# Chunks of 128 queries instead of 256 in a fused attention and FP4 feed-forward kernel, with a reordered head

## The chip, the cores and the metric

The kernel runs on one core of one Trainium2 chip. The metric is the device time of the whole program in microseconds. Engines: TensorE (PE, with its weight loads as PEld), VectorE (DVE), ScalarE (ACT), GpSimd (POOL), and SyncE (SP), which only issues transfers.

## The reference, cut to what matters

Sequence 2048, width 128, 16 heads of 8 features; all in float32.

```
x_proj = silu(x @ W1 + b1);  u, v, q, k = split(x_proj, 4)
attn   = silu(q k^T per head) / S            # no softmax, no mask
av     = attn v
y      = layernorm(av * u, gamma, beta) @ W2 + b2
x      = layernorm(x + y)
gate   = fp4(x) @ fp4(w_gate).T;  up = fp4(x) @ fp4(w_up).T      # 352 columns
h      = silu(gate) * up
out    = layernorm(x + fp4(h) @ fp4(w_down).T)
```

`fp4` quantises blocks of 16 numbers to a grid of eight magnitudes, scaled by the largest of the block.

## The kernel before, in words

**The attention.** The queries are cut into chunks (`WIDTHS`, eight of 256), and each chunk into steps (`STEPS`, 256 in all). A step has one tile of 128 keys and four head groups' worth of work, 512 columns in each of four PSUM banks: with 256 queries a step covers two of the four values of m and a chunk has 32 steps; with 128 queries it would cover all four and a chunk would have 16. Either way there are 256 steps with two ACTIVATEs (silu) of 128x1024 each.

In each step TensorE does, in this order: `scores(at)`, which is a half a=0 and a half a=1, each with bf16 matmuls of 64 rows in pairs on the two halves of the array (eight of 256 columns in a step); `times_v(at - 2)`, fp32 matmuls with 32 output columns in four column groups (sixteen records of 256 columns in a step); and then the job that `JOB_AT` has for that step, if any. A half of scores waits until ScalarE has emptied the bank pair that was used three halves ago (`SB = 3`). `times_v` waits for the ACTIVATEs of its own step.

**Jobs.** `PREP_AT` places the remaining projections (k, v, u, q), the folding of gamma and beta into W2, and the transposes of the quantised weights in steps 0 to 33. `PAIR_JOBS` places, behind the attention of the next chunk, the rest of the network for the two tiles of a finished chunk: "y" (step base + 0), "xqT" (+5), "gate" for each tile (+6, +7), "up" (+8, +9), "hqT" (+14, +15), "down" for both (+16). `PAIR_BASE` = 45, 68, 100, ... 228. A job waits until the job before it has been taken from PSUM: by ScalarE (the silu of k, q, v, u and of each "gate") or by VectorE (all others). ScalarE does its part of job(at) between its two ACTIVATEs of step at + 1. VectorE does layer norms (with a reciprocal root from GpSimd), quantisation and copies, two tiles interleaved.

**Head.** `HEAD` lists what TensorE does before step 0: transposes of x into xT and the first projections, in an order written out by hand. Biases of q and k are loaded one number to a partition by ScalarE's queue (`load_bias`), before and after the half of W1 that q and k need. VectorE permutes the columns of that half (L828). Features are split into three bf16 parts (`split`), and transfers by SyncE and GpSimd (`stack`, L231) put these into `k_stack` and `q_stack`, whose unused rows are zeroed by large transfers (`zero_rows`, L222). Step 0 waits for all of xT and for the stacks of k 0 and q 0; steps 2, 6, 10 and 14 wait for the stack of a further unit of k.

**Tail.** After the last step the last two tiles go through the whole remaining network with nothing beside them; matmuls on zeros (`KEEP_WARM`) fill TensorE's waits.

## Time and profile before

| | |
|---|---|
| median of 3 runs | 555.74 us (555.68 to 562.42) |
| the profiled execution: its own time | 553.78 us |
| its span, first to last instruction | 551.9 us |
| granted TensorE clock, mean over the span | 1.00 (2.4 GHz) |
| first attention ACTIVATE starts | 22.04 us |
| last attention ACTIVATE ends | 524.90 us |
| steps | 256, with 512 attention ACTIVATEs |

The span has three parts: a head of 22 us until the first ACTIVATE of the attention, 503 us of steps, and a tail of 27 us. Starts in the timeline are microseconds from the span's start. ACTIVATEs that follow each other overlap in the record, so their rate is read from the ends of blocks of them. Matmul records overlap too, so TensorE's steps are read from the starts of successive blocks.

### The profile page before, as it was taken

The numbers are of one execution on the slowest core, as the hardware profiler recorded it, in microseconds if no ns is written. First come the engines' busy times: TensorE is split into PE (matmuls) and PEld (weight loads), VectorE is DVE, ScalarE is ACT, GpSimd is POOL, SyncE is SP. The second block draws the span as 40 slices with busy tenths as digits, with TensorE's granted clock in tenths as the row PEclk, the third lists the DMA queues.
The fourth block names the chain that finished last, engine by engine and source line by source line (L and its number), as shares of the span: only waits on it lengthen the run. The fifth ranks groups of instructions, "written<-read, shape, count | busy, mean of one in ns | idle before, by whom it ended". The sixth has DMA issues, their size and how long they took to land.

```text
span 551.9 us, 15085 instructions
## 1 busy us (share of the span) xinstructions
PE 514.1 (93%) x6586; PEld 227.7 (41%) x6586; DVE 180.2 (33%) x610; ACT 494.3 (90%) x559; POOL 60.6 (11%) x151
## 2 busy tenths in 40 slices
PE   4699999999999999999999999999999999999996
PEld 2344444344443433434343433444343443444343
DVE  3652742043322510452023510452023510442046
ACT  2699999999999999999999999999999999999910
POOL 5840000020120010201020010201010010201021
PEclk9999999999999999999999999999999999999999
DMA  8780240000000000000000000000000000000000
GB/s 171 199 162 17 72 106 11 2 2 1 11 2 2 1 11 2 1 3 11 1 3 1 2 11 1 3 2 12 1 2 1 1 12 1 2 2 11 3 0 11
DMA packets 13993, 12.08 MB, mean 22 GB/s; under 512 B 2019, under 2 KB 13286, under 8 KB 13926
## 3 DMA queue, kind: packets, MB, share of 16 engines
q1 hardware_dynamic: 12790, 9.05, 6.8%
q0 software_dynamic: 704, 1.92, 1.5%
q8 instruction: 52, 0.85, 0.6%
q10 hardware_dynamic: 432, 0.13, 0.2%
q14 instruction: 15, 0.12, 0.1%
HBM read 1.92 MB, written 1.05 MB: 5 GB/s over the span
## 4 chain that ended last, share of the span: by engine, by line
ACT 43%; PE 30%; issue 11%; DVE 8%; POOL 4%; DMA 2%; ACTq 1%; DVEq 0%; POOLq 0%
ACT attn L573 41%; PE ps L363 28%; POOL rstd_a L357 2%; DMA b_col<-in_L_attn_b 2%; POOL rstd_b L357 2%; PE ps L507 1%; POOL ve_a L356 1%; DVE mv_a L745 1%; DVE x_b L748 1%; DVE stats_a L743 1%; DVE amax_a L712 1%; POOL ve_b L356 0%; PE ps L502 0%; ACT feat L573 0%; ACT gate_b L573 0%
## 5 line engine op out<-in xcount | busy, mean ns | idle before, releaser
L573 ACT ACTIVATE attn<-ps 128x1024 f32<-128x1024 f32 x512 | 478.2, 1146 | 18.1 <-PE ps L363 17.9
L363 PE MATMUL ps<-attn,v_pad 128*32 128x256 f32 x4096 | 273.9, 385 | 0.8 <-ACT attn L573 0.5
L363 PE MATMUL ps<-q_stack,k_stack 64*128 64x256 bf16 x2048 | 178.2, 274 | 14.7 <-ACT attn L573 0.9
L363 PEld LDWEIGHTS ps<-attn,v_pad 128*32 128x32 f32 x4096 | 107.1, 109 | 98.9 <-issue 53.4
L363 PEld LDWEIGHTS ps<-q_stack,k_stack 64*128 64x128 bf16 x2048 | 67.4, 94 | 154.0 <-ACT attn L573 115.9
L356 POOL TENSOR_TENSOR ve_a<-mv_a,eps_col 128x1 f32<-128x1 f32 x24 | 4.5, 189 | 466.3 <-DVE mv_a L745 466.3
L739 DVE SCALAR_TENSOR_TENSOR zu<-ps,uT 128x256 f32<-128x256 f32 x8 | 3.4, 423 | 121.5 <-PE ps L363 121.5
L743 DVE BATCH_NORM_STATS2 stats_a<-ps 128x6 f32<-128x128 f32 x8 | 2.4, 300 | 57.6 <-PE ps L363 57.6
L795 DVE TENSOR_TENSOR gate_a<-gate_a,ps 128x352 f32<-128x352 f32 x7 | 3.7, 522 | 50.6 <-PE ps L363 50.6
L363 PE MATMUL ps<-zeros 128*128 128x512 bf16 x75 | 18.3, 396 | 1.2 <-DVE zeros L818 1.2
L363 PE MATMUL ps<-xT,w_qk 128*128 128x512 f32 (+1 forms) x20 | 10.2, 606 | 7.9 <-DVE w_qk L828 5.5
L363 PE MATMUL ps<-wup_t,xqT 128*128 128x352 f32 x32 | 13.4, 505 | 1.8 <-ACT gate_b L573 1.8
L363 PE MATMUL ps<-wgate_t,xqT 128*128 128x352 f32 x32 | 13.4, 505 | 1.8 <-ACT gate_a L573 1.8
L680 DVE CAST parts<-feat 128x512 bf16<-128x512 f32 (+1 forms) x10 | 4.8, 476 | 30.7 <-ACT feat L573 30.7
L573 ACT ACTIVATE feat<-ps,b_col 128x512 f32<-128x512 f32 (+1 forms) x10 | 7.0, 697 | 7.5 <-PE ps L363 5.6
L357 POOL TENSOR_TENSOR rstd_b<-ve_b,minus_half 128x1 f32<-128x1 f32 x24 | 13.2, 551 | 1.9
L357 POOL TENSOR_TENSOR rstd_a<-ve_a,minus_half 128x1 f32<-128x1 f32 x24 | 13.2, 549 | 1.9
L363 PEld LDWEIGHTS ps<-zeros 128*128 128x128 bf16 x75 | 7.4, 101 | 9.8 <-issue 1.4
L641 ACT ACTIVATE xqT<-ps 128x128 f32<-128x128 f32 x2 | 0.5, 277 | 10.6 <-PE ps L554 10.6
L722 DVE TENSOR_TENSOR xn_a<-xn_a,magic_a 128x352 f32<-128x352 f32 (+3 forms) x21 | 8.5, 403 | 0.2
L721 DVE TENSOR_TENSOR xn_a<-xn_a,magic_a 128x352 f32<-128x352 f32 (+3 forms) x21 | 8.4, 401 | 0.2
L363 PEld LDWEIGHTS ps<-wup_t,xqT 128*128 128x128 f32 x32 | 4.9, 188 | 8.5 <-ACT gate_b L573 5.2
(152 smaller groups left out, 326.0 us busy)
## 6 DMA issues: line engine op xcount, KB each, us to landing
k_stack<-parts SPq DMA_DIRECT2D x18, 128.0 KB, 3.3
q_stack<-parts SPq DMA_DIRECT2D x18, 128.0 KB, 2.4
k_stack<-uT POOLq DMA_DIRECT2D x2, 448.0 KB, 7.8
q_stack<-uT SPq DMA_DIRECT2D x2, 448.0 KB, 8.2
x_sb<-in_L_attn_x SPq DMA_DIRECT2D x3, 256.0 KB, 6.9
k_stack<-parts SPq DMA_DIRECT2D x10, 64.0 KB, 3.1
q_stack<-parts SPq DMA_DIRECT2D x8, 64.0 KB, 2.0
out<-x_a SPq DMA_DIRECT2D x8, 64.0 KB, 1.5
```

What stands on the lines that cost most here:

```text
L356: link(pool.tensor_tensor(r.ve[:, :], r.mv[:, which, 1:2], eps_col[:, :], ALU.add))
L357: pool.tensor_tensor(r.rstd[:, which:which + 1], r.ve[:, :], minus_half[:, :], ALU.pow).then_inc(rstd_ready, 1)
L363: return pe.matmul(to, lhsT, rhs, start=start, stop=stop, skip_group_check=True)
L507: last = pe.transpose(ps[0:fn, bank, t * P:(t + 1) * P], r.xn[:, f0:f0 + fn], ident[:, :])
L573: return act.activation(to, frm, ACT.Silu, **kw)
L680: dve.tensor_copy(p[:, 0, :], f).then_inc(split_done, 1)
L712: each(lambda t: dve.tensor_reduce(t.amax, t.src, AX_X, ALU.max, apply_absolute_value=True))
L721: each(lambda t: dve.tensor_tensor(t.xn, t.xn, t.magic, ALU.add))
L722: each(lambda t: dve.tensor_tensor(t.xn, t.xn, t.magic, ALU.subtract))
L743: dve.bn_stats(r.stats[:, :], src)
L745: dve.bn_aggr(r.mv[:, which, :], r.stats[:, :]).then_inc(var_ready, 1)
L748: return dve.tensor_scalar(to, src, r.mv[:, which, 0:1], r.rstd[:, which:which + 1], ALU.subtract, ALU.mult)
```

## The change

- Sixteen chunks of 128 queries, sixteen steps each. A step has sixteen score matmuls of 128 columns and thirty-two records of `times_v` with 128 columns.
- One tile of 128 rows passes behind the attention beside each chunk from the second on: fifteen tiles, "y", "xqT", "gate", "up", "hqT", "down" at steps 3, 7, 9, 11, 15 and 17 from the chunk's first (the fifteenth tile: 2, 6, 8, 10, 14, 15). VectorE works on one tile at a time. The last tile alone makes the tail, with 27 and 22 zero matmuls in place of 33 and 28.
- The weights' transposes move to steps 14 to 21; the projections of q 512, 1024, 1536 and of u 1, 2, 3 move to steps 29 to 69, one for each half chunk. VectorE's program for the first chunk is laid out by steps (`QUANTISE_AFTER`).
- The head: b1 is loaded as rows on one partition, permuted by VectorE and turned into columns by three matmuls against a one; ScalarE permutes W1 in place of VectorE, and its queue issues only the load of W1's half; the columns 256 to 767 of `k_stack` are zeroed by a GpSimd memset, the rest by transfers that GpSimd issues only after its shares of the first two stacks; the order of `HEAD` has all transposes of x before v 0 and k 768.
- SyncE stacks q 512 and later units between the writes of the output.

```diff
-WIDTHS = (256,) * 8
+WIDTHS = (128,) * 16
-    KEEP_WARM = {"y": 5, "xqT": 33, "gate": 2, "hqT": 28, "down": 2}
+    KEEP_WARM = {"y": 5, "xqT": 27, "gate": 2, "hqT": 22, "down": 2}
-    PREP_AT = {0: ("k", 1280), 1: ("v", 1), 3: ("k", 1792), 5: ("v", 2), 8: ("v", 3), 10: ("u", 0),
-               12: ("q", 256), 14: ("u", 1), 16: ("q", 512), 18: ("u", 2), 20: ("u", 3), 22: ("q", 1024),
-               24: ("q", 1536), 27: ("w2", 0), 29: ("gate", 0), 31: ("up", 0), 33: ("down", 0)}
-    PAIR_BASE = [45, 68, 100, 132, 164, 196, 228]
-    PAIR_JOBS = {0: ("y", 0), 5: ("xqT", 0), 6: ("gate", 0), 7: ("gate", 1), 8: ("up", 0), 9: ("up", 1),
-                 14: ("hqT", 0), 15: ("hqT", 1), 16: ("down", 0)}
+    PREP_AT = {0: ("k", 1280), 1: ("v", 1), 3: ("k", 1792), 5: ("v", 2), 7: ("v", 3), 9: ("u", 0), 11: ("q", 256),
+               14: ("w2", 0), 16: ("gate", 0), 18: ("up", 0), 21: ("down", 0), 29: ("q", 512), 37: ("u", 1),
+               45: ("q", 1024), 53: ("u", 2), 61: ("q", 1536), 69: ("u", 3)}
+    QUANTISE_AFTER = {3: "gate", 7: "up", 11: "down"}
+    TAIL = KT - 1
+    TILE_AT = {t: (BEGIN[t + 1], {"y": 3, "xqT": 7, "gate": 9, "up": 11, "hqT": 15, "down": 17}) for t in range(TAIL - 1)}
+    TILE_AT[TAIL - 1] = (BEGIN[TAIL], {"y": 2, "xqT": 6, "gate": 8, "up": 10, "hqT": 14, "down": 15})
-        HEAD = [("xT", 0, 256, 0), ("k", 0, 256, 1), ("q", 0, 256, 2), ("xT", 256, 512, 3), ("k", 256, 512, 4),
-                ("v", 0, 512, 6), ("xT", 768, 512, 5), ("k", 768, 512, 7), ("xT", 1280, 512, 7),
-                ("xT", 1792, 256, 7)]
+        HEAD = [("xT", 0, 256, 0), ("k", 0, 256, 1), ("q", 0, 256, 2), ("xT", 256, 512, 3), ("xT", 768, 512, 4),
+                ("k", 256, 512, 5), ("xT", 1280, 512, 7), ("xT", 1792, 256, 0), ("v", 0, 512, 6),
+                ("k", 768, 512, 7)]
...
+            sp.dma_start(b1_natural[0:1, 0:2 * D], b1[2 * D:4 * D].rearrange("(a n) -> a n", a=1)).then_inc(b1_rows_loaded, 16)
+            sp.dma_start(b1u_row[0:1, 0:D], b1[0:D].rearrange("(a n) -> a n", a=1)).then_inc(b1_rows_loaded, 16)
...
+            pool.memset(k_stack[:, :, :].bitcast(F32)[:, :, 128:384], 0.0).then_inc(k_early_zeroed, 1)
...
+            pool.wait_ge(zero_row_ready, 1)
+            zero_rows(pool, k_stack, 768, k_rest_zeroed)
+            pool.wait_ge(b1v_ready, 1)
+            zero_v(0)
...
+            pe.wait_ge(b1_permuted, 1)
+            for i, row in enumerate((b1u_row[0:1, 0:D], b1_permuted_row[0:1, 0:D], b1_permuted_row[0:1, D:2 * D])):
+                last = mm(ps[:, 6, i:i + 1], row, ones_row[0:1, 0:1])
+            last.then_inc(b1_made, 1)
...
-                load_bias(2, b1k_loaded)
-                act.dma_start(w1_sb[:, 2 * D:4 * D], W1[:, 2 * D:4 * D]).then_inc(w1_kq_loaded, 16)
-                load_bias(1, b1_loaded)
+            act.dma_start(w1_sb[:, 2 * D:4 * D], W1[:, 2 * D:4 * D]).then_inc(w1_kq_loaded, 16)
...
+            def permute_w1(i):
+                src = w1_sb[:, (2 + i) * D:(3 + i) * D].rearrange("k (h s d) -> k h d s", h=2, d=HD)
+                to = w1_qk[:, i, :].rearrange("k (h d s) -> k h d s", h=2, d=HD)
+                act.activation(to, src, ACT.Copy).then_inc(w1_qk_ready, 1)
...
+            def to_quantised_x(tile):
+                r = ROWS[tile % 2]
+                bank = wait_made("y", 0, tile)
+                statistics(ps[:, bank, 0:P], 0, r)
+                y_plus_x(r, ps[:, bank, P:2 * P], tile).then_inc(job_by_vec, 1)
+                wait_taken("y", 0, tile)
+                statistics(r.x1p[:, :], 1, r)
+                quantised_x([r])
...
+            def to_out(tile):
+                r = ROWS[tile % 2]
+                bank = wait_made("down", 0, tile)
+                dve.tensor_tensor(r.x1p[:, :], ps[:, bank, 0:D], r.x1[:, :], ALU.add).then_inc(job_by_vec, 1)
+                wait_taken("down", 0, tile)
+                statistics(r.x1p[:, :], 2, r)
+                finish(tile)
```

## Rows read from the trace of the kernel before

**Rows 1.** The page: busy time of each engine; engines of the chain that ended last.

```profile
PE 514.1 (93%) x6586; PEld 227.7 (41%) x6586; DVE 180.2 (33%) x610; ACT 494.3 (90%) x559; POOL 60.6 (11%) x151
...
ACT 43%; PE 30%; issue 11%; DVE 8%; POOL 4%; DMA 2%; ACTq 1%; DVEq 0%; POOLq 0%
```

**Rows 2.** Timeline of ACT, one pair: start us, us, what, count [idle before].

```profile
234.22 1.02 ACT L573 ACTIVATE attn<-ps 128x1024 f32<-128x1024 f32 x1 [0.21 <-PE ps L363]
...
235.48 1.03 ACT L573 ACTIVATE attn<-ps 128x1024 f32<-128x1024 f32 x1
236.88 1.02 ACT L573 ACTIVATE attn<-ps 128x1024 f32<-128x1024 f32 x1 [0.36 <-PE ps L363]
...
241.87 12.94 ACT L573 ACTIVATE attn<-ps 128x1024 f32<-128x1024 f32 x14 [0.39 <-PE ps L363]
255.78 6.52 ACT L573 ACTIVATE attn<-ps 128x1024 f32<-128x1024 f32 x7 [0.98 <-PE ps L363]
```

**Rows 3.** Timeline of PE over the same pair: steps, and three jobs.

```profile
221.63 0.33 PE L502 MATMUL ps<-ident,zu 128*128 128x128 f32 x1
...
222.45 0.61 PE L363 MATMUL ps<-q_stack,k_stack 64*128 64x256 bf16 x8
...
224.00 0.61 PE L363 MATMUL ps<-q_stack,k_stack 64*128 64x256 bf16 x8
...
232.99 0.86 PE L363 MATMUL ps<-wgate_t,xqT 128*128 128x352 f32 x2
233.78 0.61 PE L363 MATMUL ps<-q_stack,k_stack 64*128 64x256 bf16 x8
...
253.81 0.94 PE L363 MATMUL ps<-wdown_t,hqT_a 128*128 128x128 f32 x6
...
255.35 0.61 PE L363 MATMUL ps<-q_stack,k_stack 64*128 64x256 bf16 x8
```

**Rows 4.** Timeline of PE in the head: a projection, then 128-column matmuls.

```profile
14.04 1.13 PE L363 MATMUL ps<-xT,w_qk 128*128 128x512 f32 x2 [1.72 <-ACT xT L604]
15.00 1.05 PE L363 MATMUL ps<-w_sb,xT 128*128 128x128 f32 x8
```

**Rows 5.** By tile, 100 to 500 us: min/median/max ns of the attention's matmuls (two answers).

```profile
L363 PE MATMUL ps<-q_stack,k_stack x1640: 268/270/282, 100.8 to 499.4; 64*128 64x256 bf16 x183
...
L363 PE MATMUL ps<-attn,v_pad x3288: 378/379/404, 99.8 to 499.9; 128*32 128x256 f32 x194
```

**Rows 6.** Timeline of PEld: the eight weight loads of one step's scores.

```profile
301.31 0.33 PEld L363 LDWEIGHTS ps<-q_stack,k_stack 64*128 64x128 bf16 x8 [0.49 <-issue]
```

**Rows 7.** Timeline of DVE: first and last instruction from "y" to quantised x.

```profile
222.56 0.30 DVE L743 BATCH_NORM_STATS2 stats_a<-ps 128x6 f32<-128x128 f32 x1 [5.86 <-PE ps L363]
...
230.67 0.29 DVE L725 TENSOR_TENSOR xn_b<-xn_b,scale_b 128x128 f32<-128x128 f32 x1
```

**Rows 8.** Timeline of the head, all engines.

```profile
0.74 1.90 ACTq L578 DMA_DIRECT2D b_col<-in_L_attn_b  x2
...
2.68 0.46 ACTq L582 DMA_DIRECT2D w_sb<-in_L_attn_W  x1
...
8.93 0.59 DVE L828 COPY w_qk<-w_sb 128x64 f32<-128x64 f32 x4 [5.37 <-DMA w_sb<-in_L_attn_W]
...
13.02 0.47 ACT L573 ACTIVATE feat<-ps,b_col 128x256 f32<-128x256 f32 x1 [1.90 <-DMA b_col<-in_L_attn_b]
...
14.12 2.35 POOL L231 DMA_DIRECT2D q_stack<-parts  x4 [0.17 <-issue]
...
22.04 2.85 ACT L573 ACTIVATE attn<-ps 128x1024 f32<-128x1024 f32 x3 [0.49 <-PE ps L363]
```

**Rows 9.** Timeline of the last steps and the tail.

```profile
515.49 9.41 ACT L573 ACTIVATE attn<-ps 128x1024 f32<-128x1024 f32 x10
...
539.17 0.52 DVE L712 TENSOR_REDUCE amax_a<-gate_a 128x22 f32<-128x352 f32 x1
...
544.62 0.53 DVE L725 TENSOR_TENSOR xn_b<-xn_b,scale_b 128x352 f32<-128x352 f32 x1
```

More of the change, by code:

```diff
@@ L96, in build, with chunk_of @@
     job_no = {job: k for k, job in enumerate(JOBS)}
[L97 to L98 removed]
+    ACT_JOBS = [k for k, (kind, i, tile) in enumerate(JOBS)
+                if kind in ("k", "q", "v", "u") or (kind == "gate" and tile is not None)]
     VEC_JOBS = [k for k in range(len(JOBS)) if k not in ACT_JOBS]
[L100 to L104 removed]
+    def chunk_of(tile):
+        return max(c for c in range(len(WIDTHS)) if Q0[c] <= tile * P)
     UNITS = [("k", 0, 256), ("q", 0, 256), ("k", 256, 512), ("k", 768, 512), ("k", 1280, 512), ("k", 1792, 256),
@@ L175, in build @@
         ROWS = [Rows([sb(f"{name}_{k}", shape) for name, shape in shapes.items()]) for k in "ab"]
+        TAIL_ROWS = [ROWS[tile % 2] for tile in range(TAIL, KT)]
         xqT = sb("xqT", [D, 2, P])
@@ L269, in _, with write_out @@
             sp.wait_ge(q_rest_zeroed, 32)
-            for n in range(unit_no[("q", 256)], len(UNITS)):
-                stack(sp, n)
-            for n in range(KT):
-                sp.wait_ge(x2_ready, n + 1)
-                sp.dma_start(out_v[:, n, :], ROWS[n % 2].x2[:, :]).then_inc(out_written[n % 2], 16)
+            stack(sp, unit_no[("q", 256)])
+            def write_out(tile):
+                sp.wait_ge(x2_ready, tile + 1)
+                sp.dma_start(out_v[:, tile, :], ROWS[tile % 2].x2[:, :]).then_inc(out_written[tile % 2], 16)
+            for at in sorted(JOB_AT):
+                kind, start, tile = JOB_AT[at]
+                if kind == "q" and start > 256:
+                    stack(sp, unit_no[("q", start)])
+                elif kind == "down" and tile is not None:
+                    write_out(tile)
+            write_out(TAIL)
             for k in range(2):
@@ L472, in job @@
                     pe.wait_ge(av_taken, STEPS[at - LAG][0])
-                if p is not None:
-                    last = behind(kind, i, p, bank)
+                if tile is not None:
+                    last = behind(kind, tile, bank)
                 elif kind == "u":
@@ new lines, in finish @@
+            def finish(tile):
+                r = ROWS[tile % 2]
+                dve.wait_ge(rstd_ready, rstd_no.next())
+                if tile >= 2:
+                    dve.wait_ge(out_written[tile % 2], 16 * (tile // 2))
+                normalise(r.x1p[:, :], r.x2[:, :], 2, r).then_inc(x2_ready, 1)
+            def to_quantised_x(tile):
+                r = ROWS[tile % 2]
+                bank = wait_made("y", 0, tile)
[4 more added lines that the diff above has]
+                quantised_x([r])
@@ new lines, in _ @@
+            for at in range(len(STEPS)):
+                if at - LAG in BEGIN[1:]:
+                    take_av(BEGIN.index(at - LAG) - 1)
+                kind, start, tile = JOB_AT.get(at, (None, None, None))
+                if tile is None:
+                    if kind in ("k", "q"):
+                        split(kind, start)
+                    elif kind == "w2":
+                        take_w2()
+                    elif kind in ("gate", "up", "down"):
+                        take_weights(kind)
+                elif kind == "y":
+                    to_quantised_x(tile)
+                elif kind == "xqT":
+                    copy_xqT(tile)
+                elif kind == "up":
+                    to_quantised_h(tile)
+                elif kind == "hqT":
+                    copy_hqT(tile)
+                elif kind == "down":
+                    to_out(tile)
+                if at in QUANTISE_AFTER:
+                    quantise_weights(QUANTISE_AFTER[at])
@@ L908, in _ @@
                 statistics(r.x1p[:, :], 2, r)
-            finish(LAST)
+            for i in range(KT - TAIL):
+                finish(TAIL + i)
 _INS = ["L0_attn_x", "L0_attn_W1", "L0_attn_b1", "L0_attn_W2", "L0_attn_b2", "L0_attn_gamma", "L0_attn_beta",
```

317 lines of the change are left out of this document (138 added, 179 removed).

## The prediction

> **What bounds the kernel now.** I read the page first: PE is busy for 93% of the span and ACT for 90%, and the chain that ended last alternates between them [rows 1]. That average does not say which waits for which, so the timeline of ACT comes next, over one pair of tiles (they repeat seven times). In an unbroken block, fourteen ACTIVATEs take 12.94 us, the first of them 1.02: (12.94 - 1.02) / 13 = 0.917 us each [rows 2]. 512 at that pace are 469 us, and nothing in the change touches it. What can be won lies outside: the head of 22.04 us until the first ACTIVATE [rows 8], the tail from 524.90 (515.49 + 9.41) to 551.9 [rows 9], and what interrupts ACT between. The first ACTIVATE ends about 1.02 after its start, at 23.06, so from there to 524.90 are 501.8 us; 511 x 0.917 = 468.3, which leaves 33.5 us of interruptions.
>
> Their kinds are seen in the same block of rows, by ends. 235.24 to 236.51 is 1.27 us, 0.35 more than the pace: the silu of "gate" that lies between, ACT's own work. 236.51 to 237.90 is 1.39, 0.47 more: a wait for PE. Six ACTIVATEs end between 235.24 and 242.89, 7.65 us, which is 2.15 over the pace: two silus (0.70) and three waits of 0.47 to 0.50 (1.45). One wait of about 0.3 stands ahead of them, and at "down" the end moves from 254.81 to 256.80, a wait of 1.07 [rows 2]. A pair thus costs 2.8 us of waits and 0.7 of silus, seven pairs 24.5. The other 9.0 lie in the first 40 steps, mostly ACT's own part of the projections.
>
> Why ACT waits is in PE's timeline. A step in which PE waits for nothing lasts 222.45 to 224.00, 1.55 us (1.544 over several), while ACT needs 2 x 0.917 = 1.833 [rows 2, 3]. PE gains 0.29 per step and loses the length of a job where one stands: "y" for two tiles 0.82, "gate" 0.79, "down" for two tiles 1.54 (253.81 to 255.35) [rows 3]. Call what PE is behind its best place the backlog. "y" with 0.82 stops ACT not at all; before "down" two "hqT" of 0.48 stand, so the backlog reaches 0.48 - 0.29 + 0.48 - 0.29 + 1.54 = 1.92, and ACT waits 1.07. So the three score buffers forgive about 0.83, and the wait is what exceeds that. Two "gate" and two "up" in four successive steps exceed it each time. Over all 256 steps this rule gives about 35 us of interruptions where the trace has 33.5, close enough to use.
>
> **The change, part by part.** *Width.* The columns streamed per step stay the same, so a gain is excluded; the number of matmuls and loads doubles. No row shows a bf16 matmul of 128 columns. Near to it are the fp32 records of 128 columns, each with a load of 128 columns of its own: eight in 1.05 us, the last 0.28, so (1.05 - 0.28) / 7 = 0.11 us each [rows 4], which is 128 columns passed twice at 2.4 GHz (0.107) and 3 ns; the load is hidden entirely. What a load costs when nothing hides it can be read from the longest matmul against the median: 12 ns for scores, 25 for times_v [rows 5], little against 56 and 110 ns of streaming. I take 3 ns per additional matmul: scores go from 4 x 0.110 to 8 x 0.056, times_v from 4 x 0.216 to 8 x 0.110, together 0.02 to 0.03, and a free step is 1.57. The lower end is 1.55. For the upper end I take the loads as they appear in a full step: eight in 0.33 us, 0.041 each [rows 6]. If the two of a pair had to run one after the other with no overlap of the matmul, a pair would last 0.083, eight 0.66, and the step 1.77.
>
> The Trainium skill ("TensorE: Matmul & The Clock Gate", section on the back-to-back issue gap) speaks against the change: it gives about 81 ns for each matmul of 128 columns in a sustained stream of loads and matmuls, against 56 for one without a load. The fp32 row above has no such addition, but its matmul is twice as long; by the page the scores would cost 8 x 0.025 = 0.2 us more and the step would be about 1.77, an estimate.
>
> *Jobs of one tile.* By records of 0.11 and 0.15 for the change of layout: "y" 0.82 - 0.33 = 0.49, "xqT" 0.26, "gate" and "up" 0.79 each as before, "hqT" 3 x 0.11 + 0.15 = 0.48, "down" 1.54 - 0.66 = 0.88; together 3.7. A chunk then asks 16 x 1.57 + 3.7 = 28.8 us of PE and 32 x 0.917 + 0.35 = 29.7 of ACT: ACT still sets the pace. With two steps between "gate" and "up" and four or more elsewhere, every job starts with little or no backlog; 0.88 after "hqT" exceeds the cushion (0.82 now) by 0.07, everything else by nothing. Fifteen tiles cost 15 x 0.07 = 1 us of waits and 15 x 0.35 = 5.3 of silus.
>
> *The last tile behind the attention* has "y" one step earlier, only one after the preceding tile's "down", and VectorE must first finish that tile (add, statistics, root, normalise) and take the chunk: about 2.6 us, against 1.57. PE waits about 1.1 us in its queue, with the scores of the next step behind it; backlog 0.6 + 1.1 + 0.49, minus 0.82, is a wait of 1.3. Its adjacent "hqT" and "down" add 0.3.
>
> *The moved projections.* One lasts 15.00 - 14.04 = 0.96 and 0.10 for layout, 1.06 [rows 4]. In the first chunks before, they stood every second step, each hidden by ACT's own work for the one before. Alone, half a chunk apart, each meets a backlog of 0.25 from the tile's job ahead: 1.31 - 0.82 = 0.5, six times 3.0. The v and k jobs of steps 0 to 9 stay about as they were, 2.0. ACT's own share of all projections is unchanged, 6.8.
>
> *Sum of interruptions:* waits 1.0 + 1.6 + 3.0 + 2.0 = 7.6, ACT's own 6.8 + 5.3 = 12.1; 19.7 against 33.5, a gain of 13.8.
>
> *Head.* W1's half for q and k is issued at 2.68 and VectorE gets it at 8.93 [rows 8], 6.2 us later. With the bias loads gone it is issued in place of the first of them, at 0.74, 1.9 earlier, and the 1.90 that ACT waited for the bias of q at 13.02 is gone too. The features of q then end near 10.3 in place of 13.5, and SyncE's and GpSimd's stacks (2.35 us of issue for GpSimd's share) with them. ScalarE pays for it with two permutations of some 0.35 us, ahead of xT. Next late is PE: all transposes, k 256, v 0 and k 768 add to 5.9 us after q, with handovers 6.5, which gives scores near 16.2 and the first ACTIVATE at 16.6 in place of 22.04: a gain of 5.4. Ends: 2 (loads land no earlier) and 7. On the other side, k_stack's rows from 768 are zeroed only after GpSimd's stacks, and SyncE's queue holds the stack of k 768 and all behind it until then; the W loads and v are late against earlier steps. I put 1 us on that, with ends 0 and 5.
>
> *Tail.* One tile in place of two. From the last ACTIVATE to the end are 27.0 us. The quantisation of h for two lasts 539.17 to 545.15, 5.98 [rows 9]; for one, the same nine durations with 0.03 between are 3.95: 2.0 gained. The same way the quantisation of x gains 0.6, the interleaved statistics 0.9, one multiplication 0.6, the second "gate" ahead of the first "up" 0.7, and the second tile's last normalisation, later than the first's, 0.8; minus overlaps and 0.5 that "down" may hold VectorE before the last take, 4.9. Ends 3.5 and 5.5.
>
> *Total:* 551.9 - 13.8 - 5.4 + 1 - 4.9 = 528.8 of span. The profiled execution took 553.78, 1.9 above its span, which gives 530.7; the median lay 2 us above the profiled execution, and I take 531.5 for the new median.
>
> **The rivals.**
>
> *Narrow loads are not hidden.* With a step of 1.77, PE asks 16 x 1.77 + 3.7 = 32.0 per chunk, 2.3 more than ACT, and PE is the bound: about 35 us over the forecast in fifteen chunks, 566. The price begins at a step of 1.63 (where 16 steps and 3.7 make 29.7), and at about 1.72 all gains are spent. For it: rows 6 as read above, and PE's small reserve. Against it: the 12 and 25 ns [rows 5] and the fp32 records [rows 4].
>
> The rule of the Trainium skill cited above (81 ns) leads to the same 1.77 and 566, an estimate.
>
> *The single tile's chain is too long.* From "y" to quantised x two tiles take 222.56 to 230.96, 8.4 us [rows 7]. For one I count 6.3, as the second tile's operations fall out between the first's; the step of "xqT" comes 6.5 after "y" (four steps less the backlog). If the chain stayed at 8.4, PE would stand 2.0 us at each "xqT" with scores behind it: 2.0 + 0.26 - 0.82 = 1.4, fifteen times 21, so 552, no difference. What speaks for it is that each VectorE operation waits for the one before and nothing fills the gaps; against it, the root's round trip and the gaps are counted.
>
> *The head gives its gain back*: ACT starts at 16.6 but waits in steps 2 to 18 for stacks, v or quantised weights as long as it started early. 531.5 + 5.4, up to 540.
>
> **Chances.** Forecast (525 to 536) 0.55; the head's gain lost or half of some other term (536 to 544) 0.20; the chain, or PE a little over its reserve (544 to 556) 0.09; narrow loads (over 556) 0.12; better than 525 0.04. For 8 in 10 the range needs the first two and most of the third: 525 to 552. A measurement of this kernel tells 2% from no change, 544.6 below and 566.9 above; faster 0.79, within 0.13 (the third case and a third of the fourth), slower 0.08.
>
> **What would show it.** Right: free steps near 1.57 in PE's timeline; ACT in unbroken blocks of nearly a chunk, broken by the silu alone; waits of 0.5 at six projections; one wait over 1 us at step 242; the first ACTIVATE before 18 us; a tail of 22 us. Wrong: blocks of scores that last over 0.7 us where nothing holds them; PE idle before "xqT" until VectorE's last operation in every chunk; waits for transfers in the first chunk.

## The result, and the profile after

The changed kernel takes 535.57 us (median of four runs, 532.63 to 536.49), the kernel before 557.41 beside it (555.68 to 562.42): a ratio of 0.959, 95% interval 0.952 to 0.966, 22 us less. Its profiled execution took 532.63 us with a span of 530.5; 551.9 stood before. The forecast was 528.8 for the span, 531.5 for the median.

The page of the changed kernel, the rows that answer to [rows 1], and the queue that fetches instructions:

```profile
PE 511.4 (96%) x12724; PEld 378.3 (71%) x12724; DVE 210.8 (40%) x627; ACT 492.5 (93%) x558; POOL 63.3 (12%) x152
...
q8 instruction: 100, 1.64, 1.3%
...
ACT 43%; PE 42%; issue 10%; DVE 3%; POOL 1%; DMA 1%; POOLq 0%; DVEq 0%; ACTq 0%
```

TensorE has twice the instructions and 3 us less of busy time; VectorE, GpSimd and the DMAs have 5% of the chain together, where they had 14%.

Where the 21.4 us of span came from, by the three stretches of the prediction. The pace of 0.917 us per ACTIVATE is the same in both; an interruption is what the ends of successive ACTIVATEs lie apart beyond it. The prediction took 468.3 for 511 paces, and 511 x 0.917 is 468.6; to stay comparable the table and all sums of interruptions below keep its figure, so that each is 0.3 too high and the differences are not touched:

| stretch | before | after | change | forecast |
|---|---|---|---|---|
| start of the first ACTIVATE | 22.04 | 16.74 | -5.3 | -5.4 |
| interruptions of ACT | 33.5 | 21.7 | -11.8 | -13.8, and +1 given back |
| end of the last ACTIVATE to the end | 27.0 | 22.8 | -4.2 | -4.9 |

*One chunk.* Timeline of PE in the changed kernel, parts of steps 67 to 79 (start us, us, engine, line, what, count):

```profile
123.11 0.33 PE L530 MATMUL ps<-ident,zu 128*128 128x128 f32 x1
...
123.59 0.62 PE L385 MATMUL ps<-q_stack,k_stack 64*128 64x128 bf16 x16
...
125.15 0.62 PE L385 MATMUL ps<-q_stack,k_stack 64*128 64x128 bf16 x16
125.70 1.08 PE L385 MATMUL ps<-attn,v_pad 128*32 128x128 f32 x32
126.71 1.12 PE L385 MATMUL ps<-xT,w_sb 128*128 128x512 f32 x2
127.77 0.62 PE L385 MATMUL ps<-q_stack,k_stack 64*128 64x128 bf16 x16
...
134.86 0.86 PE L385 MATMUL ps<-wgate_t,xqT 128*128 128x352 f32 x2
135.66 0.62 PE L385 MATMUL ps<-q_stack,k_stack 64*128 64x128 bf16 x16
...
146.88 0.55 PE L535 MATMUL ps<-ident,xn_a 128*128 128x128 f32 x3
147.36 0.72 PE L385 MATMUL ps<-q_stack,k_stack 64*128 64x128 bf16 x16
```

The free step is 125.15 - 123.59 = 1.56 us, against 1.55 with columns twice as wide [rows 3]: twice as many loads and matmuls cost 0.01. The jobs are the distances to the scores behind them: "y" 0.48, a projection 1.06, "gate" 0.80, "hqT" 0.48.

Timeline of ACT in the changed kernel, two places in the middle, then the last two chunks and a half:

```profile
117.56 10.30 ACT L599 ACTIVATE attn<-ps 128x1024 f32<-128x1024 f32 x11
128.21 1.02 ACT L599 ACTIVATE attn<-ps 128x1024 f32<-128x1024 f32 x1 [0.35 <-PE ps L385]
...
144.19 1.02 ACT L599 ACTIVATE attn<-ps 128x1024 f32<-128x1024 f32 x1 [0.28 <-PE ps L385]
...
439.52 26.82 ACT L599 ACTIVATE attn<-ps 128x1024 f32<-128x1024 f32 x29
466.22 0.48 ACT L599 ACTIVATE gate_b<-ps 128x352 f32<-128x352 f32 x1
466.56 15.78 ACT L599 ACTIVATE attn<-ps 128x1024 f32<-128x1024 f32 x17
483.46 12.02 ACT L599 ACTIVATE attn<-ps 128x1024 f32<-128x1024 f32 x13 [1.12 <-PE ps L385]
495.36 0.48 ACT L599 ACTIVATE gate_a<-ps 128x352 f32<-128x352 f32 x1
495.70 12.05 ACT L599 ACTIVATE attn<-ps 128x1024 f32<-128x1024 f32 x13
```

Blocks of 29 where there were blocks of seven and fourteen [rows 2]. The rows at 128.21 and 144.19 are the waits at projections, 0.46 and 0.39 by the ends. The row with 1.12 idle is the last tile's "y" at step 242; by the ends, as the prediction counts, it is (483.46 + 1.02) - (466.56 + 15.78) - 0.917 = 1.22, against 1.3. Timeline of PE at that place:

```profile
482.56 0.30 PE L530 MATMUL ps<-ident,zu 128*128 128x128 f32 x1 [0.97 <-DVE zu L764]
```

TensorE stands 0.97 us in its queue for VectorE, where the prediction had 1.1.

*The head.* Rows of several engines of the changed kernel, against [rows 8]:

```profile
0.74 0.42 ACTq L601 DMA_DIRECT2D w_sb<-in_L_attn_W  x1
...
3.37 0.43 ACT L623 ACTIVATE w_qk<-w_sb 128x128 f32<-128x128 f32 x1 [0.68 <-DMA w_sb<-in_L_attn_W]
...
16.74 2.86 ACT L599 ACTIVATE attn<-ps 128x1024 f32<-128x1024 f32 x3 [0.55 <-PE ps L385]
...
22.61 1.02 ACT L599 ACTIVATE attn<-ps 128x1024 f32<-128x1024 f32 x1 [1.53 <-PE ps L385]
...
34.83 1.94 ACT L599 ACTIVATE attn<-ps 128x1024 f32<-128x1024 f32 x2 [1.48 <-PE ps L385]
```

W1's half, issued at 0.74, is usable at 3.37. Of the wait of 1.53, 0.6 is for a stack of k, which the prediction had on its list (TensorE stands 0.58 for it); kernels below that wait for no stack there still show 0.89. The 1.48 was on no list. Timeline of PE at that place:

```profile
31.04 1.08 PE L385 MATMUL ps<-attn,v_pad 128*32 128x128 f32 x32
32.05 0.34 PE L385 MATMUL ps<-q_stack,k_stack 64*128 64x128 bf16 x6
34.56 0.45 PE L385 MATMUL ps<-q_stack,k_stack 64*128 64x128 bf16 x10 [2.17 <-issue]
```

TensorE stops for 2.17 us after the sixth of sixteen score matmuls. The program has a wait before the first and the ninth, none before the seventh. ACT loses 1.58 there by the ends and 0.76 more at the next step (1.04, where four kernels without such a stop at that place have 0.28), 2.3 in all.

*The tail.* Timeline of DVE in the changed kernel: from "y" to quantised x, and the quantisation of h:

```profile
510.98 0.30 DVE L768 BATCH_NORM_STATS2 stats_b<-ps 128x6 f32<-128x128 f32 x1 [1.05 <-PE ps L385]
...
516.97 0.29 DVE L750 TENSOR_TENSOR xn_b<-xn_b,scale_b 128x128 f32<-128x128 f32 x1
...
520.12 0.52 DVE L737 TENSOR_REDUCE amax_b<-gate_b 128x22 f32<-128x352 f32 x1
...
523.65 0.53 DVE L750 TENSOR_TENSOR xn_b<-xn_b,scale_b 128x352 f32<-128x352 f32 x1
```

The chain of one tile lasts 517.26 - 510.98 = 6.28 us (forecast 6.3; two tiles took 8.4 [rows 7]), the quantisation 4.06 (forecast 3.95).

### The profile page after: what moved, and what is told of

It is laid out like the page before. It is cut to its first block, busy times and chain, and to the rows that moved or that the text cites. A ratio compares the mean times of both kernels' runs of the same rounds, so it can differ in the third digit from the quotient of the medians.

```text
span 530.5 us, 27409 instructions
## 1 busy us (share of the span) xinstructions
PE 511.4 (96%) x12724; PEld 378.3 (71%) x12724; DVE 210.8 (40%) x627; ACT 492.5 (93%) x558; POOL 63.3 (12%) x152
## 3 DMA queue, kind: packets, MB, share of 16 engines
q8 instruction: 100, 1.64, 1.3%
HBM read 1.92 MB, written 1.05 MB: 6 GB/s over the span
## 4 chain that ended last, share of the span: by engine, by line
ACT 43%; PE 42%; issue 10%; DVE 3%; POOL 1%; DMA 1%; POOLq 0%; DVEq 0%; ACTq 0%
ACT attn L599 41%; PE ps L385 39%; PE ps L535 1%; PE ps L530 1%; DMA k_stack<-parts 1%; PE ps L417 1%; ACT feat L599 0%; POOL rstd_b L373 0%; ACT gate_a L599 0%; ACT gate_b L599 0%; DVE parts L705 0%; DVE magic_b L848 0%; DVE stats_b L768 0%; POOL rstd_a L373 0%; ACT uT L599 0%
## 5 line engine op out<-in xcount | busy, mean ns | idle before, releaser
L385 PE MATMUL ps<-attn,v_pad 128*32 128x128 f32 x8192 | 276.5, 276 | 0.0
L385 PEld LDWEIGHTS ps<-attn,v_pad 128*32 128x32 f32 x8192 | 208.1, 109 | 26.6
L385 PE MATMUL ps<-q_stack,k_stack 64*128 64x128 bf16 x4096 | 170.2, 218 | 8.3 <-issue 2.2
L385 PEld LDWEIGHTS ps<-q_stack,k_stack 64*128 64x128 bf16 x4096 | 115.0, 94 | 80.9 <-ACT attn L599 42.7
L372 POOL TENSOR_TENSOR ve_b<-mv_b,eps_col 128x1 f32<-128x1 f32 x24 | 4.6, 190 | 210.5 <-DVE mv_b L770 210.5
L818 DVE TENSOR_TENSOR gate_b<-gate_b,ps 128x352 f32<-128x352 f32 x7 | 3.6, 521 | 55.3 <-PE ps L385 55.3
L385 PE MATMUL ps<-zeros 128*128 128x512 bf16 x63 | 15.7, 399 | 1.2 <-DVE zeros L839 1.2
L385 PE MATMUL ps<-wgate_t,xqT 128*128 128x352 f32 x32 | 13.7, 511 | 0.0
L705 DVE CAST parts<-feat 128x512 bf16<-128x512 f32 (+1 forms) x10 | 6.3, 632 | 14.5 <-ACT feat L599 14.5
L773 DVE TENSOR_SCALAR x_b<-x1p_b,mv_b,rstd_b 128x128 f32<-128x128 f32 x16 | 5.5, 346 | 14.9 <-POOL rstd_b L373 14.9
L773 DVE TENSOR_SCALAR x_a<-x1p_a,mv_a,rstd_a 128x128 f32<-128x128 f32 x16 | 5.5, 346 | 14.9 <-POOL rstd_a L373 14.9
```

The costliest lines, as they stand in the source:

```text
L372: link(pool.tensor_tensor(r.ve[:, :], r.mv[:, which, 1:2], eps_col[:, :], ALU.add))
L385: return pe.matmul(to, lhsT, rhs, start=start, stop=stop, skip_group_check=True)
L705: dve.tensor_copy(p[:, 0, :], f).then_inc(split_done, 1)
L773: return dve.tensor_scalar(to, src, r.mv[:, which, 0:1], r.rstd[:, which:which + 1], ALU.subtract, ALU.mult)
L818: dve.tensor_tensor(r.gate[:, :], r.gate[:, :], ps[:, bank, 0:FF], ALU.mult).then_inc(job_by_vec, 1)
```

## The experiments

My theory was that of the prediction: TensorE's backlog with a cushion of about 0.8 us decides what a job costs, narrow loads are free, the new head brings 4.4 us net. Medians of the changed kernel itself differ by 2 us from one set to the other (535.57 and 533.37), so effects of 1 or 2 us are read from the timelines. The rivals were narrow loads that cost, a chain that is too long, and a head that gives its gain back. The kernel before ran beside each set: 556.37 us beside the first four kernels, 556.14 beside the next four, 557.02 and 556.16 beside the last. Ratios are to it, with 95% intervals.

**The width alone undone.** Chunks of 256 again, one tile per sixteen steps, the new head; the tail has two tiles and its longer runs of zero matmuls.

```
-WIDTHS = (128,) * 16
+WIDTHS = (256,) * 8
-    TAIL = KT - 1
+    TAIL = KT - 2
-    TILE_AT = {t: (BEGIN[t + 1], {"y": 3, "xqT": 7, "gate": 9, "up": 11, "hqT": 15, "down": 17}) for t in range(TAIL - 1)}
+    TILE_AT = {t: (BEGIN[t // 2 + 1] + 16 * (t % 2), {"y": 3, "xqT": 7, "gate": 9, "up": 11, "hqT": 15, "down": 17})
+               for t in range(TAIL - 1)}
```

> Chunks of 256 queries as before, but everything else as after the change: one tile at a time behind the attention, a job at most every second step, the new head. As a chunk of 256 ends two tiles at once, fourteen tiles pass behind the attention and two make the tail. Theory (the gain between head and tail comes from the spacing of the jobs, and the width itself gives nothing): free steps of 1.54 us, interruptions of ACT about 20 us as after the change (21.7), the tail back at 27, so a span near 534.5 where the changed kernel's is 530.5. Rival (the narrower chunk gives the gain between): interruptions near 33 us as before and a span near 546. Second rival (narrow matmuls cost something hidden in the sum): interruptions under 16 us, a span near or under 530.

532.88 us, 0.957 (0.954 to 0.960). The span is 532.1, 2.4 less than expected: first ACTIVATE 17.34, interruptions 17.9 (between the theory's 20 and the 16 of the second rival), tail 27.5. The narrow chunks themselves thus bring the tail (4.7 us) and cost about as much in interruptions (21.7 against 17.9): a wash. The 3.8 can be found in the timelines of ACT: steps 7 and 8, with the stop of 2.17 us that only the changed kernel has, 2.4; the wait at the last "y", 1.23 against 0.20; the six projections 0.8, since they wait 0.23 to 0.38 here and 0.39 to 0.46 there; one tile fewer behind the attention, with its silu and smaller waits at "down", 0.7. Against these, steps 1 and 2 lose 1.05 more here, with TensorE at half clock from 18.1 to 24.9 us. What this experiment shares with the change, single tiles spread over sixteen steps and the head, is where nearly all of the gain lies.

**The new head alone** (all that the change does ahead of the steps), with the width, the pairs of tiles and the positions of all jobs as before; against the changed kernel:

```
-WIDTHS = (128,) * 16
+WIDTHS = (256,) * 8
...
+    PAIR_BASE = [45, 68, 100, 132, 164, 196, 228]
+    PAIR_JOBS = {0: ("y", 0), 5: ("xqT", 0), 6: ("gate", 0), 7: ("gate", 1), 8: ("up", 0), 9: ("up", 1),
+                 14: ("hqT", 0), 15: ("hqT", 1), 16: ("down", 0)}
```

> The kernel before with the new head alone. Theory: the first ACTIVATE of the attention at 16.7 in place of 22.0 us, 1 to 3 us of it given back in the first ten steps to late stacks, all later steps as before: 2.5 to 4.5 us less than before. Rival (the transfers of the first 38 us are what bounds the start, so the gain is given back): less than 1 us. Other rival (nothing is given back): 5.3 us.

549.95 us, 0.988 (0.985 to 0.991), 6.4 us less; the span 547.4 is 4.5 less. The first ACTIVATE starts at 16.59 (5.45 earlier), the interruptions are 34.5 (1.0 more, nearly all at step 2), the tail the same 26.96. So the head gives back 1.0, the figure that the prediction took. From this kernel to the one with the width undone, 549.95 to 532.88 us, the interruptions fall from 34.5 to 17.9 at the same width: that is the spacing of the jobs, with the projections moved.

**"up" right behind "gate"**, a step of distance less:

```
-    TILE_AT = {t: (BEGIN[t + 1], {"y": 3, "xqT": 7, "gate": 9, "up": 11, "hqT": 15, "down": 17}) for t in range(TAIL - 1)}
+    TILE_AT = {t: (BEGIN[t + 1], {"y": 3, "xqT": 7, "gate": 9, "up": 10, "hqT": 15, "down": 17}) for t in range(TAIL - 1)}
```

> The changed kernel with "up" one step after "gate" in place of two, for fourteen tiles. Theory (waits come from backlog beyond the score buffers' cushion of 0.82 us, and an adjacent job also waits for ACT's silu): a wait of 0.4 to 0.5 us at each, 14 x 0.47 = 6.6 us slower than the changed kernel. Rival (only the sum of PE's work per chunk counts, 28.8 us against 29.7 for ACT): no difference.

540.66 us, 0.973 (0.968 to 0.977). ACT waits 0.47 more at each of the fourteen tiles, 6.6 in all; a shorter pause at 37 us takes 1 of it back, and the span is 535.7, 5.2 more. By the rule, backlog after two jobs of 0.79 is 0.79 - 0.29 + 0.79 = 1.29, which exceeds the cushion of 0.83 by 0.46. One step of distance is worth 5 us, and the rival that only the sum of the work counts is out. The agreement to 0.01 is partly luck. Timeline of PE of this kernel:

```profile
197.58 0.62 PE L385 MATMUL ps<-q_stack,k_stack 64*128 64x128 bf16 x16
199.47 0.86 PE L385 MATMUL ps<-wup_t,xqT 128*128 128x352 f32 x2 [0.26 <-ACT gate_a L599]
```

TensorE also stands 0.26 us before each "up" until ACT has done the silu of "gate", which the rule leaves out. It leaves out the silu's 0.35 us of ACT in the same step too, which gives TensorE time, and the two nearly cancel.

**Scores cut into 64 columns**, 32 matmuls and 32 loads per step in place of 16:

```
-                            last = mm(ps[:, bank + half, k * w:(k + 1) * w],
-                                      k_stack[rows, M * a + m, i * P:(i + 1) * P],
-                                      q_stack[rows, M * a + m, Q0[c]:Q0[c] + w])
+                                lo, hi = part * (w // 2), (part + 1) * (w // 2)
+                                last = mm(ps[:, bank + half, k * w + lo:k * w + hi],
+                                          k_stack[rows, M * a + m, i * P:(i + 1) * P],
+                                          q_stack[rows, M * a + m, Q0[c] + lo:Q0[c] + hi])
```

> The changed kernel with each score matmul of 128 columns cut in two of 64, each with its own weight load (32 in a step). Theory A (a pair costs its columns and 3 ns, loads hidden): a free step of 1.60, under 3 us slower. Theory B (loads of a pair overlap each other but take 0.041 us each pair at least): scores 16 x 0.041 = 0.66, a free step of 1.77 and 30 us slower. Theory C (0.041 for each load, one after another): scores 1.3 us, a free step of 2.4 and some 200 us slower.

542.75 us, 0.975 (0.971 to 0.979). Timeline of PE of this kernel, a free step:

```profile
203.65 0.64 PE L385 MATMUL ps<-q_stack,k_stack 64*128 64x64 bf16 x32
204.22 1.08 PE L385 MATMUL ps<-attn,v_pad 128*32 128x128 f32 x32
205.24 0.64 PE L385 MATMUL ps<-q_stack,k_stack 64*128 64x64 bf16 x32
```

1.59 us: even loads followed by only 64 columns are hidden but for 0.03 per step, as theory A had it. Its "under 3 us slower" was wrong: the median is 7 us above the changed kernel's, the span 10.9. That is no regular cost. The first ACTIVATE is 1.05 later, and the interruptions are 31.4, 9.7 more. Seventeen times TensorE stops inside a block where the program has no wait, like the stop of 2.17 us above: 0.23 to 2.63 us from the start of one matmul to the next, 9.1 together. Two stretches of 3.4 us at half clock come on top, one behind the first scores and one behind the stop of 2.63.

**"xqT" a step earlier**, so that VectorE's chain is late:

```
-    TILE_AT = {t: (BEGIN[t + 1], {"y": 3, "xqT": 7, "gate": 9, "up": 11, "hqT": 15, "down": 17}) for t in range(TAIL - 1)}
+    TILE_AT = {t: (BEGIN[t + 1], {"y": 3, "xqT": 6, "gate": 9, "up": 11, "hqT": 15, "down": 17}) for t in range(TAIL - 1)}
```

> The changed kernel with "xqT" three steps after "y" in place of four, for fourteen tiles. Theory (a single tile's chain from "y" to quantised x takes 6.3 us, and the step comes about 4.8 us after "y"): PE stands 1.6 us at each "xqT", and ACT waits 1.6 + 0.26 - 0.82 = 1.0 to 1.1 us, 14 to 16 us slower than the changed kernel. Rival (the chain of one tile takes as long as that of two, 8.4, and was hidden only just): 3 us each, over 40 us slower. Rival (the score buffers cover it): no difference.

550.73 us, 0.989 (0.981 to 0.996). Timeline of PE of this kernel:

```profile
194.19 1.08 PE L385 MATMUL ps<-attn,v_pad 128*32 128x128 f32 x32
197.00 0.30 PE L550 MATMUL ps<-ident,xn_a 128*128 128x128 f32 x1 [1.73 <-DVE xn_a L750]
197.23 0.62 PE L385 MATMUL ps<-q_stack,k_stack 64*128 64x128 bf16 x16
197.78 1.40 PE L385 MATMUL ps<-attn,v_pad 128*32 128x128 f32 x32
```

TensorE stands 1.73 us in its queue with the scores behind it, and ACT loses 1.22 in each chunk that has no projection: 1.73 + 0.26 - 0.82 = 1.17 by the rule. Where a projection stands between "y" and "xqT", as in steps 55 and 71, the loss is 0.18. This is the rival of the long chain, made real: the margin in the changed kernel is less than one step. The fourth row of the fence, 1.40 for what elsewhere takes 1.08, shows more: TensorE goes to half clock behind the pause, from 198.4 to 201.8 us (mean granted clock 0.93 from 188 to 200 us), and ACT loses another 1.5 us here, and as much again near step 200, behind the same pause. Behind the eight other pauses of this length the clock stays up.

**Tile 13 a step earlier at its end**, so that the last tile's "y" finds VectorE free:

```
+    TILE_AT[TAIL - 2] = (BEGIN[TAIL - 1], {"y": 3, "xqT": 7, "gate": 9, "up": 11, "hqT": 14, "down": 16})
```

> The changed kernel with "hqT" and "down" of the fourteenth tile one step earlier (14 and 16), so that VectorE has two steps between that "down" and the "y" of the fifteenth tile. Theory: the one wait of 1.2 us at step 242 goes, 1.2 us faster. Rival (the wait is for the attention's own product, not for VectorE's queue): no difference.

531.54 us, 0.955 (0.949 to 0.961). The wait at step 242 is gone. Timeline of ACT of this kernel, one block over both chunks where the changed kernel had 1.12 idle:

```profile
466.83 27.69 ACT L600 ACTIVATE attn<-ps 128x1024 f32<-128x1024 f32 x30
```

So its cause was VectorE, still on the tile before, as TensorE's row at 482.56 has it. The edit is worth 1.2 us; the medians differ by more (4.0 and 1.8 from those of the changed kernel), and nothing shows the rest to be its doing.

**All zeroing by memset** instead of transfers of a zero row:

```
-            zero_rows(sp, q_stack, 256, q_rest_zeroed)
...
-            pool.memset(k_stack[:, :, :].bitcast(F32)[:, :, 128:384], 0.0).then_inc(k_early_zeroed, 1)
+            pool.memset(k_stack[:, :, :].bitcast(F32)[:, :, 128:512], 0.0).then_inc(k_early_zeroed, 1)
...
-            zero_rows(pool, k_stack, 768, k_rest_zeroed)
...
+            dve.memset(k_stack[:, :, 1024:1536], 0.0)
...
+            dve.memset(k_stack[:, :, 1536:2048], 0.0).then_inc(k_rest_zeroed, 1)
...
+                    for n in range(7):
+                        last = dve.memset(q_stack[:, :, 256 * (n + 1):256 * (n + 2)], 0.0)
```

> The changed kernel with all zeroing by memset (GpSimd and VectorE, in stretches where they idle) in place of transfers, 1.5 MB of the about 5.5 MB that move in the first 38 us. Theory (the waits of 1.6, 1.6 and 1.0 us in steps 2, 7 and 8 come from transfers that are crowded: the stack of k 256 landing late, and a pause of 2.4 us within a block of matmuls that no semaphore explains, laid to the fetching of instructions): 2.5 to 4 us faster, and no pause within a block. Rival (the pause has nothing to do with the transfers): the pause stays, at most 1.5 us faster. Rival (the memsets hold up splits or GpSimd's copies as much): no difference or slower.

531.5 us, 0.954 (0.948 to 0.959): interruptions 20.1 in place of 21.7, and no pause inside a block. That is 1.6 us where 2.5 to 4 were expected: the pause with what follows it is gone (2.3) and step 2 is 0.4 shorter, but steps 3, 4 and 6 now wait 0.3 to 0.5 each, with half clock from 21.9 to 25.3 us.

**Both of the last two edits together.**

> The two preceding edits together. If they are independent: the sum of their gains, 3.7 to 5.2 us faster than the changed kernel.

529.04 us, 0.950 (0.946 to 0.954), the best of the study beside a later one. First ACTIVATE 16.85, interruptions 18.3, tail 22.8. The interruptions are 3.4 fewer than in the changed kernel, 1.8 and 1.6 for the two edits by themselves: they add up. Timelines of DVE and POOL in its head:

```profile
18.26 2.15 DVE L701 CAST parts<-feat 128x512 bf16<-128x512 f32 x1
...
22.23 0.43 DVE L701 CAST parts<-feat 128x512 bf16<-128x512 f32 x1
```

```profile
18.32 1.80 POOL L313 MEMSET v_pad<- 128x2048 f32 x1
```

The same CAST takes 0.43 us, or 2.15 beside a memset of GpSimd's, and ends 0.28 us after it.

**The changed kernel again**, unaltered, beside the next two.

> The changed kernel once more, unaltered, on the chip of the two kernels beside it. By every theory: 0.955 to 0.962 of the kernel before, some 533 to 536 us, the first ACTIVATE of the attention at 16.7 to 17.3 us, 1.2 us of waiting at step 243, and at least one pause of TensorE inside a block of sixteen score matmuls in the first 40 us.

533.37 us, 0.959 (0.954 to 0.963), with the first ACTIVATE at 17.75, later than every theory had it. Timeline of PE in its head:

```profile
13.64 1.02 PE L385 MATMUL ps<-xT,w_qk 128*128 128x512 f32 x2
17.11 1.04 PE L385 MATMUL ps<-q_stack,k_stack 64*128 64x128 bf16 x16 [2.44 <-DMA q_stack<-parts]
18.07 1.22 PE L385 MATMUL ps<-xT,w_qk 128*128 128x512 f32 x1
```

The first scores take 1.04 in place of 0.62: from 16.8 to 20.3 us the granted clock is at its lower level, after TensorE had waited for the stacks. In the first profile of the same program TensorE waited 0.84 us there, for ACT, the clock did not fall, and the first ACTIVATE stood at 16.74. Of the 1.01 us between the two, 0.81 is the start of the scores (16.30 and 17.11, the landing of q's stack) and 0.2 the clock. The program's six executions here, ordered by mean granted clock:

```
clock  1.000  0.998  0.997  0.996  0.992  0.991
span   528.6  530.6  531.6  531.2  533.3  533.9
```

A mean clock that is lower by 0.009 is 0.009 x 530 x 2 = 9.5 us at the lower level, which costs half of that, 4.8, if TensorE bounds the kernel; 5.3 are seen. The changed kernel's spread thus goes with TensorE's clock. That of the kernel before does not: beside these six, its spans of 555.2 and 553.9 us had clocks of 1.000 and 0.991.

**GpSimd zeroes v_pad before it issues stacks**, on top of both edits, to keep its memset away from the CASTs of 2.15 us:

```
+            zero_v(0)
+            zero_v(1)
             pool.wait_ge(stack_zeroed, 2)
             for n in range(2):
                 stack(pool, n, SHARES[n][1], by_pool=True)
...
-            zero_v(0)
...
-            zero_v(1)
```

> The kernel with the later jobs of tile 13 and all zeroing by memset (529.0 us), and now GpSimd zeroes both halves of v_pad before it issues its share of the stacks, so that no memset of its runs beside VectorE's two CASTs. My theory (the memset beside them is what stretches the CASTs from 0.43 to 2.0 us each): the CASTs at 0.4 to 0.5 us, what waits for them 1 to 2 us earlier, the median 527.5 to 528.5. The rival (the CASTs are not on the path, and GpSimd's stacks are now issued later): CASTs short, but the second steps wait as before or 0.4 to 1 us longer, the median 529 to 530. If the CASTs stay at 2.0 us, the memset was not the cause.

533.67 us, 0.958 (0.955 to 0.961), 4.6 us worse than both edits alone. Neither theory saw it. The CASTs behind are short, but the memset now lies beside an earlier one:

```profile
10.08 1.40 DVE L701 CAST parts<-feat 128x256 bf16<-128x256 f32 x1
...
14.51 0.43 DVE L701 CAST parts<-feat 128x512 bf16<-128x512 f32 x1
```

That CAST leads to GpSimd's share of k's stack, whose issue moves from 10.89 to 12.14 us, and q's behind it from 12.14 to 13.39. TensorE, done at 14.5, waits 3.97 us for q's stack, and then the windows of this kernel show (busy us of each engine, then granted clock, DMA share, GB/s):

```profile
14.00:18.00 4.00, 0.54 (x2) 0.00 (x0) 3.74 (x7) 1.00 (x2) 3.96 (x7) 0.82 0.85 219
18.00:22.00 4.00, 3.49 (x30) 1.82 (x32) 0.00 (x0) 1.94 (x2) 4.00 (x8) 0.50 0.95 230
22.00:26.00 4.00, 2.73 (x19) 2.06 (x15) 2.13 (x4) 2.52 (x3) 1.26 (x3) 0.50 0.88 227
```

Half clock for 10 us, from 16.6 to 26.8 by the records of the granted clock. The stretching does follow the memset; it was harmless where it had been, and costly where I put it.

**The same with TensorE warmed up**, eight zero matmuls at the start and two more behind the first transposes:

```
-    WARM_UP = 5
+    WARM_UP = 8
+    if n == 0:
+        for _ in range(2):
+            mm(ps[:, 7, :], zeros[:, 0:P], zeros[:, :])
```

> The kernel beside it with eight in place of five matmuls of zeros ahead of the head's work, and two more behind the first transposes of x. My theory: TensorE's granted clock is at its upper level (2.4 GHz) from some 7 us on instead of from 12 to 13 us, the projections of the head take half their time, and the first ACTIVATE of the attention starts up to 1.7 us earlier: 526 to 528 us. First rival: the clock stays at the lower level in the head and the extra matmuls only cost their time, up to 1 us slower. Second rival: the landing of the stacks bounds the first ACTIVATE, so that the projections are shorter and nothing else moves.

533.86 us, 0.958 (0.954 to 0.962). TensorE's clock rises at 4.8 us in place of 9.8 and its head's work is done 2 us earlier, but the same CAST is stretched to 2.81 us, the stacks come later still, TensorE waits 6.96 us and is at half clock for 13.7. The second rival held, with this on top: work that ends earlier in front of a transfer only lengthens the wait, and the wait takes the clock.

**Both edits, warmed up and kept busy**: GpSimd's order as in the changed kernel, and eighteen more zero matmuls ahead of the first scores.

```
             pe.wait_ge(head_act, xT_all)
+            for _ in range(18):
+                mm(ps[:, 3, :], zeros[:, 0:P], zeros[:, :])
```

> The kernel of 529.0 us (later jobs of tile 13, all zeroing by memset) with TensorE kept busy through the head: eight matmuls of zeros at the start in place of five, two more behind the first transposes of x, and eighteen ahead of the first scores, where TensorE waited for the stacks 2.4 us in the changed kernel, 4.0 and 7.0 us in the last two kernels, and ran at half clock for 3.4, 10.2 and 13.7 us after it. My theory (TensorE's wait for the stacks lets its clock fall, in some runs and not in others, and each microsecond at half clock costs half a microsecond): no stretch at half clock before the end of the attention in any profile, mean granted clock 0.997 or more, the first ACTIVATE at 16.2 to 17.0 us, all runs within 1.5 us of one another, the median 527.5 to 529. Rival: the zeros are late themselves and hold the first scores up, the first ACTIVATE 1 us or more later, 530 us or more. Second rival: the half-clock stretches have another cause, they come all the same in some runs, and the runs spread over 3 us or more as those of the changed kernel did.

529.06 us, 0.952 (0.950 to 0.955). Timeline of PE of this kernel:

```profile
12.44 4.05 PE L381 MATMUL ps<-zeros 128*128 128x512 bf16 x18
16.86 0.62 PE L381 MATMUL ps<-q_stack,k_stack 64*128 64x128 bf16 x16 [0.38 <-DMA q_stack<-parts]
```

No half clock in this profile from 5.1 us to the tail, and executions between 528.77 and 530.48, a spread of 1.7 against 5.3 in the changed kernel's six. But the median is that of both edits alone, and so nearly is the spread (528.29 to 530.37): there TensorE waited only 1.03 us for the stacks and its profile shows no fall of the clock either. Two of the five executions still had a mean clock of 0.996 and 0.997, by the sum above some 3 to 4 us at the lower level, so the zeros did not end the falls everywhere; the second rival is weakened and not out. The first ACTIVATE, at 17.30, is later than I expected: the landing of q's stack at 16.8 bounds it, not the zeros.

**What the pauses inside blocks are.** The instruction queue q8 carries TensorE's program: 64 bytes for each of its instructions (matmuls and loads) are 2 x 6586 x 64 = 0.84 MB in the kernel before, where the page has 0.85; 2 x 12724 x 64 = 1.63 in the changed one, which has 1.64; 2.15 and 2.16 with 64-column scores. It comes in packets of 16 KB, 256 instructions, 2.7 steps. In the changed kernel one begins at 31.68 us and ends at 33.03, and TensorE goes on at 34.56, 1.5 us later. The same distance, from the end of such a packet to the end of a pause, for every place in a block of scores or `times_v` where two matmuls start over 0.22 us apart with no wait of the program between them (a pause is that distance of starts here):

```
kernel                 pauses          us from packet's end to the next matmul
changed (two runs)     2.4, 2.1        1.53, 1.60
"up" behind "gate"     1.3             1.43
"xqT" earlier          1.3, 1.8        1.74, 1.68
tile 13 earlier        1.5             1.34
both edits             0.9             1.41
64 columns             17, 0.2 to 2.6  1.22 to 1.61
```

Packets are 4 to 5 us apart in steady state, so 24 pauses that all end within 0.5 us of the same distance are no chance, and the kernels with half as many instructions (the one before, with the width undone, with the head alone) have none over 0.23 at the upper clock. The reading that fits is that TensorE ran out of instructions. Why a packet comes late is not shown. Before its pause the changed kernel shows a gap of 9.9 us between two packets, at 21.80 and 31.68, but the kernel kept busy with zeros has one of 9.5 (18.17 to 27.63) and no pause. The DMA engines are full between 30 and 38 us (share 1.06) where the zero rows are written, and all six profiles of kernels with narrow matmuls and these transfers have a pause at 29 to 39 us; of the five kernels without them (all by memset) four have none over 0.3 us, but one has 0.9, with a DMA share of 0.24 there.

## Why the prediction held, point by point

- **Narrow loads.** Right: 1.56 against 1.57. The Trainium skill's figure for a sustained stream (about 81 ns per matmul of 128 columns; "TensorE: Matmul & The Clock Gate", back-to-back issue gap) is refuted for this pattern: sixteen matmuls in two row halves begin every 34 ns, a pair every 69 by (125.70 - 125.15) / 8, and at 64 columns nothing collapses.
- **Jobs of one tile.** Right: 0.48, 0.26, 0.80, 0.79, 0.48 and 0.87 against 0.49, 0.26, 0.79, 0.79, 0.48 and 0.88; ACT waits 0.06 at each "down", forecast 0.07.
- **The rule of backlog and cushion.** Right, and tested at three places: 0.47 against 0.46 ("up" earlier, where two terms that the rule leaves out cancel), 1.22 against 1.17 ("xqT" earlier), 1.22 against 1.3 (step 242, gone with its cause).
- **Projections.** 0.39 to 0.46 each against 0.5, with 0.23 to 0.38 in wide chunks: 2.6 in all against 3.0.
- **Sum of interruptions.** 21.7 against 19.7 and 1 given back. Of the 1.0, 0.3 is the slip in 511 x 0.917. That only 0.7 is left is luck in part: the pause at 32 us costs 2.3, and the waits forecast elsewhere were 1.7 too high together (the projections 0.4, the last tile 0.4, "down" 0.4, the first steps 0.5). An instruction stream that runs dry stood in none of my rivals.
- **Head.** Right: 16.74 and 16.59 against 16.6, and 1.0 given back. I had PE as next late, which holds in the first profile, where the first scores wait for ACT's part of PE's last projection. In the second profile of the same program, and in the eleven other kernels with this head, they wait for q's stack, which comes between 16.1 and 19.5 us: 16.6 is among the early cases, and the start varies between 16.7 and 17.8 in the same program.
- **Tail.** 4.2 against 4.9 of gain. The two chains measured were within 0.1. The rest lies in three terms: from the last multiplication of x's quantisation to "gate" times "up" 0.4 in place of 0.7, from the end of h's quantisation to the end 0.4 in place of 0.8, and VectorE, busy with the tile before, takes the last chunk 0.7 later in place of 0.5.
- **Median.** 535.6 against 531.5, the largest miss: 1.7 is the span of the profiled execution. I gave the median 0.8 over the profiled execution, where it is 2.9: that execution had a mean clock of 0.997, the others 0.989 to 0.992. The term that was mis-sized is that of run to run, and it goes with the clock: 0.0065 x 533 us is 3.5, by the sum above.

## What to carry to other kernels

Where two engines are nearly balanced, write down how much the slower one's buffers forgive (here 0.83 us) and what a step gives back (0.29), and place jobs by it: one step of distance was worth 5 us, halving the matmuls' width cost and gave about as much. Before moving work in a head, ask what it will lie beside and which transfer waits for it, and look at the granted clock behind each wait of TensorE. Count a program's instructions as traffic too: with twice as many, ACT lost 2.3 us to what looks like their fetch, and it showed itself only as a pause at a place where the code has no wait.
